# Recurrence of a GRU: 28 of the 48 small products of a step written over 32 columns, 28 of which get zeros

## The reference, cut to what matters

```python
def step(h, xs):                      # h: [4, 256], xs: products of the input, [4, 256] each
    xzt, xrt, xht = xs
    z = sigmoid(xzt + h @ U_z + vz)
    r = sigmoid(xrt + h @ U_r + vr)
    hh = tanh(xht + r * h @ U + vh)
    h_new = (1.0 - z) * h + z * hh
    return (h_new, h_new)
_, out_t = lax.scan(step, h0, xs)     # 512 steps in turn
x = x + ffn(out_t)                    # FFN with exact GELU, then kept or not by a top-k of the scores
x = x + moe64(moe4(x, cond))          # the two mixtures of experts
```

## Time and profile before

| | |
|---|---|
| median of 3 runs | 2125.25 us (2121.49 to 2125.89) |
| the profiled execution: its time, its span | 2127.46 us, 2125.4 us |
| busy, share of the span: TensorE, its weight loads | 98%, 93% |
| busy: VectorE, ScalarE, GpSimd | 74%, 48%, 20% |
| mean granted TensorE clock | 0.754 of full speed |
| matmuls in the program's run | 32737 |

### The profile page before, as it was taken

One profiled execution on the slowest core, in us unless ns is written; L12 is line 12 of the kernel. 1 busy time (PEld: TensorE's weight loads), 2 busy tenths in 40 slices (PEclk: granted clock), 3 DMA queues, 4 the chain that ended last, 5 costly groups with the idle time before them and its releaser, 6 DMA issues. The chain is left out here.

```text
span 2125.4 us, 80897 instructions
## 1 busy us (share of the span) xinstructions
PE 2088.2 (98%) x32737; PEld 1966.4 (93%) x32737; DVE 1572.2 (74%) x9004; ACT 1028.3 (48%) x3981; POOL 416.7 (20%) x560
## 2 busy tenths in 40 slices
PE   8999999999999999999899999999999999999997
PEld 7899999999999999999768888767999999999997
DVE  7887878887887887888745555593777777777775
ACT  4665565665665665656555767533222222222221
POOL 0000000000000000000000000444555555555553
PEclk6555555555555555555599999999999999999999
DMA  3001000000000000000003222314888888888882
GB/s 127 4 4 44 4 4 4 4 4 4 4 4 4 4 4 4 4 4 4 3 0 121 87 80 80 128 49 155 283 275 282 268 271 284 268 269 282 273 264 58
DMA packets 55542, 213.59 MB, mean 100 GB/s; under 512 B 11578, under 2 KB 40960, under 8 KB 46976
## 3 DMA queue, kind: packets, MB, share of 16 engines
q1 hardware_dynamic: 36276, 184.41, 23.7%
q0 software_dynamic: 17408, 23.61, 6.0%
q10 hardware_dynamic: 1484, 0.40, 0.1%
HBM read 192.82 MB, written 15.57 MB: 98 GB/s over the span
## 5 line engine op out<-in xcount | busy, mean ns | idle before, releaser
L1900 PE MATMUL bank<-xe,ring 128*128 128x160 f32 x3072 | 438.7, 299 | 0.7 <-DVE xe L1958 0.7
L1900 PEld LDWEIGHTS bank<-xe,ring 128*128 128x128 f32 x3072 | 422.7, 190 | 0.9 <-issue 0.9
L1951 DVE STREAM_TRANSPOSE turned<-ye 32x64 f32<-32x64 f32 x1240 | 291.0, 235 | 16.1
L871 PEld LDWEIGHTS bank<-keep_part,Us 128*128 128x128 f16 x6120 | 273.4, 111 | 0.4 <-issue 0.4
L1664 POOL MEMSET cum<- 128x320 f32 x1 | 0.4, 365 | 1341.4 <-POOLq L1056 1341.4
L871 PE MATMUL bank<-keep_part,Us 128*128 128x4 f16 x6120 | 255.5, 169 | 0.0
L1936 ACT ACTIVATE gate_f<-bank 128x160 f32<-128x160 f32 x384 | 116.9, 305 | 282.4 <-PE bank L1900 279.8
L871 PE MATMUL bank<-raw,Us 128*128 128x4 f16 x6132 | 242.2, 167 | 1.5 <-issue 1.5
L1841 POOL DMA_INDIRECT out_rows<-res,to_row x128 | 192.4, 1503 | 242.0 <-issue 227.8
L514 ACT ACTIVATE r_h<-bank 128x8 f32<-128x8 f32 x512 | 93.3, 182 | 275.7 <-PE bank L871 275.2
L1911 PE MATMUL bank<-mid,ring 128*128 128x160 f32 x1536 | 219.1, 299 | 0.0
(11 more groups left out here) (281 smaller groups left out, 4059.4 us busy)
## 6 DMA issues: line engine op xcount, KB each, us to landing
ring<-in_ew SPq DMA_DIRECT2D x64, 2304.0 KB
raw<-in_L_cond_ew SPq DMA_DIRECT2D x16, 1024.0 KB, 6.3
ctx_rows<-rows SPq DMA_DIRECT2D x2, 1280.0 KB, 7.0
dense_w<-in_L_ffn_W SPq DMA_DIRECT2D x2, 1024.0 KB, 9.5
dense_w<-in_L_cond_sw SPq DMA_DIRECT2D x2, 1024.0 KB, 6.4
out_rows<-res,to_row POOLq DMA_INDIRECT x128
xT<-in_xT SPq DMA_DIRECT2D x2, 864.0 KB, 10.6
dense_w<-in_sw1T SPq DMA_DIRECT2D x1, 1536.0 KB, 10.8
```

The lines of the kernel that those rows point to most:

```text
L871: last = nc.tensor.matmul(pre[g][q][:, jj, m, :], Us[:, g, p, k, m * P:(m + 1) * P], x[part][:, k * B:(k + 1) * B], start=False, stop=Fals ...
L1900: last = nc.tensor.matmul(bank[f % UPS][:, s_ * CAP:(s_ + 1) * CAP], w1[u][:, k, s_ * FFN + f * P:s_ * FFN + (f + 1) * P], xe[e % 2][:, k] ...
L1951: last = nc.vector.transpose(y[:, :, q, :], ye[e % 2][q * SQ:(q + 1) * SQ, :, j * SQ:(j + 1) * SQ])
```

## The change

The tiles `rh_high`, `step_high` and `keep_part` get 8 times as many elements (`WIDTH` = 8); what is behind the first 8 stays zero from a memset at the start (VectorE has one memset more, and three larger ones). A new function `recur_wide` issues the same products with the same weights as `recur` did for the high part of r (8), for the high part of the candidate (8) and for both parts of (1 - z) * h (12). Its moving operand has n = min(8, 40 - jj) pieces of 4 columns, the first real and the others zeros, and its output has the 4 columns of this step and half and those of the same half of the n - 1 steps behind it, to which zeros are added. The pieces of the output lie 8 columns apart, those of the operand 8 x 3 elements (`rh_high`, `step_high`) or 8 elements (`keep_part`). The products of z (12) and those of the low parts of r and of the candidate (8 together) stay as they were. The number of instructions of TensorE, ScalarE, GpSimd and the DMA queues and their order are the same.

```diff
--- before.py
+++ after.py
@@ -242,14 +242,17 @@
         scale = t("scale", [P, 3 * GATES + 1])
         ring = t("ring", [P, 2 * SEG, C2])
         nz, keep, step_in = t("nz", [P, C2]), t("keep", [P, C2]), t("step_in", [P, C2])
-        keep_part = t("keep_part", [P, 2, C2], F16)
+        WIDTH = 8
+        keep_wide = t("keep_part", [P, 2, WIDTH * C2], F16)
+        keep_part = keep_wide[:, :, 0:C2]
         tz, lift = t("tz", [P, C2]), t("lift", [P, 1])
         half_c, turn_c = t("half_c", [P, KD, B]), t("turn_c", [P, KD, B])
         peak4, peak3 = t("peak4", [P, 3, KH]), t("peak3", [P, 3])
         fpeak, fdiag = t("fpeak", [3, 1]), t("fdiag", [3, 3])
 
         r_h, z_cand = t("r_h", [P, C2, 3]), t("z_cand", [P, C2, 3])
-        rh_high, step_high = t("rh_high", [P, C2, 3], F16), t("step_high", [P, C2, 3], F16)
+        rh_wide, step_wide = t("rh_high", [P, WIDTH * C2, 3], F16), t("step_high", [P, WIDTH * C2, 3], F16)
+        rh_high, step_high = rh_wide[:, 0:C2], step_wide[:, 0:C2]
         rh_low, step_low = t("rh_low", [P, C2, 3], F16), t("step_low", [P, C2, 3], F16)
         r, nz_one = r_h[:, :, 1], nz[:]
         z, cand = z_cand[:, :, 1], z_cand[:, :, 2]
@@ -545,12 +548,12 @@
                 nc.vector.memset(ring[:, 2 * SEG - 1], 0.0).then_inc(s_h, 1)
                 nc.vector.memset(part_of(0, -1), 0.0).then_inc(s_hhi, 1)
                 nc.vector.memset(part_of(1, -1), 0.0).then_inc(s_hlo, 1)
-                for f in (r_h, z_cand, rh_high, step_high, step_low):
+                for f in (r_h, z_cand, rh_wide, step_wide, step_low, keep_wide):
                     nc.vector.memset(f[:], 0.0).then_inc(s_zero, 1)
-                dve.wait_ge(s_zero, 5)
+                dve.wait_ge(s_zero, 6)
                 nc.vector.memset(rh_high[:, :, 0:2], -1.0).then_inc(s_zero, 1)
                 nc.vector.memset(step_high[:, :, 0], -1.0).then_inc(s_shi, 1)
-                dve.wait_ge(s_zero, 6)
+                dve.wait_ge(s_zero, 7)
                 dve.sem_inc(s_slo, 1)
 
                 def low_inputs(span, pieces):
@@ -860,7 +863,11 @@
                 nc.tensor.matmul(bank[1][:, GATES * C2:GATES * C2 + GATES * KD], bias_rows[:], ident[0:GATES * KD, 0:GATES * KD],
                                  start=True, stop=True, skip_group_check=True).then_inc(s_v, 1)
 
-                kept = [keep_part[:, p] for p in range(2)]
+                def wide_of(v):
+                    return v.rearrange("p (i c) -> p i c", c=C2)
+
+                kept_wide = [wide_of(keep_wide[:, p]) for p in range(2)]
+                reset_wide, step_w = wide_of(rh_wide[:, :, 2]), wide_of(step_wide[:, :, 2])
                 reset = [rh_high[:, :, 2], rh_low[:, :, 2]]
                 step = [step_high[:, :, 2], step_low[:, :, 2]]
 
@@ -872,6 +879,15 @@
                                                         x[part][:, k * B:(k + 1) * B],
                                                         start=False, stop=False, skip_group_check=True)
                     return last
+
+                def recur_wide(g, q, jj, x, part):
+                    n = min(WIDTH, SPAN - jj)
+                    for m in range(KD):
+                        for k in range(KD):
+                            for p in PART_OF[part]:
+                                nc.tensor.matmul(pre[g][q][:, jj:jj + n, m, :], Us[:, g, p, k, m * P:(m + 1) * P],
+                                                 x[:, 0:n, k * B:(k + 1) * B],
+                                                 start=False, stop=False, skip_group_check=True)
 
                 def ffn_up(window, n):
                     span, f, i = window - 1, n // TERMS, n % TERMS
@@ -933,7 +949,7 @@
                             pe.wait_ge(s_ulo, 1)
                         if m > 1:
                             pe.wait_ge(s_shi, m)
-                            recur(0, q, jj, step, 0)
+                            recur_wide(0, q, jj, step_w, 0)
                             pe.wait_ge(s_slo, m)
                             recur(0, q, jj, step, 1).then_inc(s_rp, 1)
                         if m == 2:
@@ -960,7 +976,7 @@
                             pe.wait_ge(s_ulo, 3)
                         if m > 1:
                             pe.wait_ge(s_rhhi, m)
-                            recur(2, q, jj, reset, 0)
+                            recur_wide(2, q, jj, reset_wide, 0)
                             pe.wait_ge(s_rhlo, m)
                             recur(2, q, jj, reset, 1).then_inc(s_cp, 1)
 
@@ -984,9 +1000,9 @@
                             if njj == 0:
                                 pe.wait_ge(s_seed, (span + 1) * GROUPS * B)
                             pe.wait_ge(s_khi, m)
-                            recur(0, nq, njj, kept, 0)
+                            recur_wide(0, nq, njj, kept_wide[0], 0)
                             pe.wait_ge(s_klo, m)
-                            recur(0, nq, njj, kept, 1)
+                            recur_wide(0, nq, njj, kept_wide[1], 1)
                         if m == S:
                             keep_busy(nc, bank[5], ones_bf, idle_rows[:], 4)
```

## The result

The changed kernel takes 2142.83 us (median of 4 runs, 2141.77 to 2143.72) against 2125.57 us for the one before, measured beside it. The ratio is 1.0084, with a 95% interval of 1.0072 to 1.0095: slower by 0.84%, some 18 us. The forecast was no change, and the time lies 5 us above the stated range.

The account below looks back on a forecast made before the run. The prediction took the recurrence's latency chain through TensorE, ScalarE and VectorE as the bound. Its terms, 0 + 0 + 0, left the profiled 2127.5 us unchanged, 2125.5 us against the median; range 2111 to 2138 us.

Parts of the forecast that it names:

- The bound: Recurrence: each step is a latency, a chain through TensorE, ScalarE and VectorE, at TensorE's lower clock, 0.50.
- two places: TensorE on the path: next span's input product, some 13 ns a step; third wide product ahead of keep_part, some 35.
- The price of a wide product: 28 products a step: 32 columns need 26.7 ns, hidden under the 27.5 ns load; price zero, upper end +4.5 us.
- The cushion of r: r's group of 8 high products: its low products wait for VectorE's scan anyway, so longer high products add nothing.
- count of 432 and 132 steps: Steps where candidate's 8 and keep_part's 12 products would count: 5040 products, 5.0 us per ns above 27.5.
- strides: Operands of r and candidate 3 elements apart: columns taking twice as long, 0.4 us a step, some 2330 us; chance 0.05.
- Slower: the columns are longer than the load: Candidate's 8 high and keep_part's 12 products: 5.0 us per ns, 2138 us at 30 ns; chance 0.20.
- The clock: TensorE in the recurrence: no rise from 0.50 expected; released, 2105 us throughout or 2115 us half the time, chance 0.27.
- The value of a step: Recurrence step at the full clock: 1.987 us less 20 ns for eight low products, so 1.97 us.
- 20 us for a full clock throughout: Whole kernel: some 19 us from recurrence steps plus 1.6 us behind it, giving 2105 us; chance 0.07.

Follow-up runs that it names:

- the three kernels with more columns: Changed kernel, wider, mostly on side-by-side zeros: all 48 products at 32 columns 2115.99 us, 28 at 64 columns 2126.66 us, all 48 at 64 columns 2145.42 us.
- the last kernels above: Changed kernel with z's products widened too, strided ones at 24 columns: others at 48 columns 2120.49 us; zeros also ahead of real pieces 2115.17 us.
- six kernels: Changed kernel widened: all 48 products at 32 or 64 columns, 28 at 64; z's products also widened, at 48, 64, or 48 with zeros ahead; 2115.17 to 2145.42 us.

## Why the prediction was wrong

**The bound.** Right: the recurrence is a chain through three engines, TensorE late in two places. All the time lost was lost in the steps.

**The price of a wide product.** Here it failed: "I take 26.7 ... the columns hide under the load of the next product, and the pace stays 27.5. Price zero". That was one column a cycle from rows whose operands lie side by side, used for two operands that don't. It holds for keep_part, 26.7 ns a product. (The loads' own pace was 26.7 too; the 27.5 had one longer gap among its 12. So columns and load were as long as each other, and side by side that cost nothing.) For the 16 products of step_high and rh_high the third or fourth of eight and those behind it follow one another at 32 to 33 ns; that is 28 ns more for step_high's group (0.24 to 0.27 us) and 16 to 20 for rh_high's (its load row 0.26 to 0.28), whose second product comes sooner than before.

**The cushion of r.** "For r the group of 8 has a cushion" was right about its kind, wrong to be left without a size. The low products of r wait for the scan, which lets them start 0.24 us behind the high ones; the eight high ones, at a pace of 26.7 ns, are through at 0.23. So there was 0.01 us to spare, and the group grew to 0.27. About half of the 0.03 comes back within the low products, which now stand ready: 0.11 us from step_low to z's group where it took 0.12 to 0.13.

**Where it counted.** So both groups came onto the path. With the first step of a span as step 0, a step grew by some 40 ns in the steps 1 to 27; in 28 to 31, where three products of 160 columns leave neither group any cushion, by 75; in 32 by 33; in 33 to 38, with 28 columns or fewer, by nothing. The last 31 steps, without a product of the next input, grew by 24. In all it is 17.6 us. The prediction's count of 432 and 132 steps took the products as wide up to the end of a span, where they aren't.

**The rivals.** The one named "strides", at 0.05, is what happened, with the right operands and groups, and only its size was off: I took double the time, 53 ns, some 200 us, with nothing between that and no price at all. The measured 32 to 33 ns is over a fifth more than 26.7. Half of the rule of the Trainium skill that stood there (Advanced Engine Details and Errata, Memory Cachelines) can be told now: its part on PSUM does not bite on pieces of four columns, since keep_part writes such pieces at the old pace. Its part on SBUF asks for two accesses to a line of 16 bytes; elements 6 bytes apart mostly meet that, and cost over a fifth all the same at 32 columns, nothing at 28. "Slower: the columns are longer than the load" put the candidate's group on the path, rightly, but keep_part's for r's, and by the length of the columns alone.

**The clock.** Right that it stays at 0.50, with the change. The rule that activity releases it (the Trainium skill, TensorE: Matmul & The Clock Gate, Part 1) holds for zeros also, as the three kernels with more columns show. The value of a step was near: 1.96 to 1.97 us at the full clock in the last kernels above, forecast 1.97. Of the 20 us for a full clock throughout none got more than some 10, at a clock of 0.90 over the recurrence.

## What to carry to other kernels

A matmul of few columns has room for more under its weight load, and those are free only while the pace stays that of the loads; before using that room, look at how the moving columns lie, since a price read from side-by-side operands doesn't hold for others. A wait that covers a group has a size, and it is to be read before the group is called covered. A low TensorE clock can be lifted by columns that add nothing, but a half measure buys nothing: it pays when it holds, and when it doesn't lengthen the last product before a wait. If two groups differ in a profile though their shapes are the same, compare their access patterns first.

## What the runs showed of the hardware

- 32 float16 moving columns that lie 3 elements apart took 32 to 33 ns a product where 32 side by side took 26.7, at the low clock; 28, 24 and 16 of them hid under the load, at 26.9. VectorE's work beside them made no difference.
- Columns of zeros released TensorE's clock from 0.50 to 1.00 for most of the recurrence in six kernels (mean 0.84 to 0.93), and the full clock made a step of 2.00 us only 0.03 to 0.04 shorter.
- The clock behind the recurrence changes at other places from one profiled execution to another: the same six products behind the same idle time took 2.93 us once and 1.68 another time, with nothing changed there.
